# The small network and its border products in two batches, the first beside the last image's attention output; constant tables loaded as two parts by casting DMAs

## The chip, the cores and the metric

One core of a Trainium2 chip runs the whole program. The metric is the device time of one execution in microseconds, lower is better.

## The reference

Input x is [8, 128, 32, 32], f32. Two blocks follow each other (B = 8 images, C = 128 channels, N = 1024 positions):

```
# block 1, self-attention, per image
hn  = groupnorm(x, 16 groups) * norm_w + norm_b
q, k, v = conv1x1(hn; wq,bq), conv1x1(hn; wk,bk), conv1x1(hn; wv,bv)      # [128, 1024]
att = softmax(q^T k * C**-0.5)                                            # [1024, 1024]
x1  = x + conv1x1(v att^T; wp, bp)
# block 2, filter in the Fourier domain, on x1
xf   = fftshift(fft2(x1, ortho));  mag = mean over channels of |xf|
c    = mag[b, centre 7x7].reshape(8, 49)
par  = relu(c @ w1 + b1) @ w2 + b2                                        # the small network: 3 numbers an image
kern = an anisotropic Gaussian, 7x7, from par (an angle by arctan2, two widths by exp), over its sum + 1e-8
out  = real(ifft2(ifftshift(wr (kern * xf)))) + x1                        # zero-padded 7x7 convolution of xf
```

## The kernel before, in words

**Block 2 without a Fourier transform.** A circular convolution of the spectrum is a product in image space with a small function KHAT of the position; what zero padding changes is a correction of low rank. So for each image the kernel computes a feature row R = (projections of x1, 448 columns, and 50 columns with the real and imaginary parts of the central frequencies), then the 49 kernel values, KHAT as one product of the kernel with a cosine table, the correction through small matrices G and G3, Z = KHAT * X1 + correction, and the output as mix(Z) + X1.

**Precision.** Products are done in f32r on operands split into a high and a low part (QH and QL, ETH and ETL, SYH and SYL, ...): three passes, hi*hi, hi*lo, lo*hi. ACT rounds the high part off (a Copy into the f32r tile), and DVE or POOL subtracts it from the full value for the low part. This holds for the constant tables too: `ana` (features, tiles ANH and ANL), `syn` (SYH and SYL; its last 1024 columns are the cosine table), `gam` (border matrices GAMR and GAM3R, whose middle 32 rows are the low part). SP loads them in f32 and the engines split them.

**Engines and queues.** Every engine has its own program, in order; a wait on a semaphore holds all that is queued behind it. Names: `p_`, `a_`, `v_`, `g_` semaphores are raised by TensorE (PE), ACT, DVE, POOL, and `d_` by DMAs.

**Attention.** `attention(run, eng)` calls `image(b, cur, prev, nxt)` for b = 0, then in a loop for 1 to 6, then for 7, and a ninth time with cur = False for what is left of image 7. An image has eight tiles t of 128 queries: TensorE scores(t); DVE row maximum (L1080); ACT exponential (L814); DVE reciprocal of the row sum; POOL scale (L1446, 128x1024, in place in E); TensorE transposes (L450); ACT and DVE the high and low parts ETH (L823) and ETL (L1095); values(h, c) as products with V. Between the tiles stand the last steps of the image before: out_hi (L792) and out_lo (L1107), out_project, residual (DVE, T, L1116), x1_transposes (L495), XTH (L829) and XTL (L1100), keep_x1 (POOL, L1451), and at its end analysis(p) (`features` of 8 tiles, L504), whose result ACT copies to R (L921).

**The ninth call.** It has no scores. TensorE does values(7,0,2), transposes(7,7), values(7,0,3), values(7,1,0), out_project(7,0), values(7,1,1), x1_transposes(7,0), values(7,1,2), rt(0), values(7,1,3), out_project(7,1), four tiles of features, x1_transposes(7,1), the other four, and r3(0). ACT and DVE split the synthesis table in the meantime (L899, L900; L1226, L1230).

**The small network for all 8 images at once**, when R is complete: DVE squares and adds (L1246, L1248), ACT root, TensorE channel mean, DVE copy (C), TensorE hidden, DVE (HIDV), TensorE parameters, then `params` and `mlp_kernel` on DVE: some 33 operations on 49 x 8 to 49 x 32 elements of the tile ML (L1285 to L1346), each followed by a wait for its own result where the next one needs it, with a square root and an exponential on ACT in the middle. Then ACT the exponential of the kernel, TensorE its sum, DVE the quotient K (L1353), TensorE and both engines K3, the kernel in three parts. The borders are 14 products with 16 columns and 49 with 8:

```
for i in range(2 * NZ):
    ins = mm(bank(5)[0:CH, i * 2 * B:(i + 1) * 2 * B], GAMR[:, i * CH:(i + 1) * CH], K3[:], True, True)
ins.then_inc(s["p_g"], 1)
for i in range(NK):
    ins = mm(bank(4)[0:NK, i * B:(i + 1) * B], GAM3R[:, i * NK:(i + 1) * NK], K3[:, 0:B], True, True)
ins.then_inc(s["p_g"], 1)
```

DVE copies the first 14 (g_columns, L1361) and multiplies out G of image 0 (g_full, L1129) while the 49 run, then g3_columns (L1372).

**Synthesis.** `first()` and eight calls of `step(i, more)`, those for i = 1 to 4 in a loop. In a step TensorE does z(i,0), r3(i+1), z(i,1), v3(i+1), khat(i+1, 0 and 1), vt(i+1), mix(i,0), rt(i+2) (L526), mix(i,1). DVE does z_sum (L1161), g_lo, v3_lo, g_full, g3_copy (L1137), vt_lo, result(i,0) (L1170), rt_lo(i+2) (L1122), result(i,1), of which z_sum, v3_lo and vt_lo free TensorE. ACT does the high parts and the two copies of KHAT (L851), POOL KHAT * X1 (L1471), the low part of Z (L1477) and two copies for rt (L1461, L1463). TensorE's mix(i,1) goes to PSUM bank 7, and result(i,1) raises v_o to 2i + 2.

All matrix products have line L386, all plain low parts in the synthesis L1122, all plain ACT copies there L856.

## Time and profile before

| | |
|---|---|
| three runs | 463.03, 463.01, 457.34 us (median 463.01) |
| the profiled execution | 462.83 us |
| its span, first to last instruction | 461.0 us |
| busy in the span | PE 413.8, PEld 347.8, DVE 318.4, ACT 254.1, POOL 232.7 us |
| mean granted TensorE clock | 0.939 |

Rows and timeline entries give microseconds from the span's start; busy time of TensorE is at whatever clock was granted then, where 1.00 is 2.4 GHz and 0.50 is 1.2 GHz.

### The profile page before, as it was taken

Reading aid. Unit: us, or ns where it says so; the run is one execution under the profiler, and the core shown is the slowest. Engines: PE = TensorE matmul, PEld = TensorE weight load, DVE = VectorE, ACT = ScalarE, POOL = GpSimd, SP = SyncE. Lnnn points to the kernel's source line nnn. Section 1 sums busy time; section 2 is a strip of 40 time slices with the busy share of each in tenths; the row PEclk is TensorE's granted clock in tenths of the full one; section 3 lists DMA queues with packets and bytes.
Section 4 is the critical chain, followed back from the end, with each engine's and each line's share of the span. In section 5 each row is a group of like instructions: output and inputs, shape, how many; then the busy total and the mean of one; then the engine's idle time right before and its main releaser. Section 6 shows DMA issues by size and latency. Waiting matters only on the chain.

```text
span 461.0 us, 7023 instructions
## 1 busy us (share of the span) xinstructions
PE 413.8 (90%) x2263; PEld 347.8 (75%) x2263; DVE 318.4 (69%) x575; ACT 254.1 (55%) x450; POOL 232.7 (50%) x169
## 2 busy tenths in 40 slices
PE   2679899999999999999999999999965089999996
PEld 2458688888788888878888887888844088888884
DVE  3569689768849967894995889478353832577765
ACT  1557676656747665774665677467512312355551
POOL 0566457636816753781673477176013512467562
PEclk9989999999999999999999999999988555599999
DMA  6900100100000010010001001001150000111112
GB/s 173 376 30 2 46 1 0 47 0 0 11 35 0 0 45 0 0 45 0 0 0 45 0 0 46 1 1 43 71 132 0 0 1 1 45 46 45 67 71 91
DMA packets 6095, 17.54 MB, mean 38 GB/s; under 512 B 1633, under 2 KB 2273, under 8 KB 5857
## 3 DMA queue, kind: packets, MB, share of 16 engines
q1 hardware_dynamic: 4784, 16.70, 10.7%
q10 hardware_dynamic: 1296, 0.66, 0.5%
q8 instruction: 8, 0.13, 0.1%
q14 instruction: 7, 0.05, 0.0%
HBM read 13.16 MB, written 4.19 MB: 38 GB/s over the span
## 4 chain that ended last, share of the span: by engine, by line
PE 34%; issue 28%; POOL 25%; DVE 7%; ACT 3%; DMA 1%; POOLq 1%
PE PS L386 28%; POOL E L1446 17%; POOL VL L1436 4%; POOL HNL L1432 3%; PE PS L504 3%; PE PS L450 2%; POOL X L1451 1%; DMA X<-in_x 1%; DVE K L1353 1%; PE PS L526 1%; ACT E L814 1%; DVE NMX L1080 1%; DVE ETL L1095 1%; DVE ML L1285 1%; ACT ETH L823 0%
## 5 line engine op out<-in xcount | busy, mean ns | idle before, releaser
L1446 POOL TENSOR_TENSOR E<-E,RI 128x1024 f32<-128x1024 f32 x64 | 124.6, 1947 | 117.3 <-DVE RI L1085 117.3
L1080 DVE TENSOR_REDUCE NMX<-PS 128x1 f32<-128x1024 f32 x64 | 77.9, 1217 | 35.7 <-PE PS L386 35.2
L814 ACT ACTIVATE E<-PS,NMX 128x1024 f32<-128x1024 f32 x64 | 71.5, 1116 | 35.9 <-DVE NMX L1080 35.8
L823 ACT ACTIVATE ETH<-PS 128x512 fp32r<-128x512 f32 x128 | 69.5, 596 | 35.9 <-PE PS L450 35.5
L1095 DVE TENSOR_TENSOR ETL<-PS,ETH 128x512 fp32r<-128x512 f32 x128 | 82.1, 683 | 8.5 <-ACT ETH L823 7.7
L450 PE MATMUL PS<-MISC,E 128*128 128x128 f32 x512 | 67.6, 275 | 3.0 <-POOL E L1446 2.1
L450 PEld LDWEIGHTS PS<-MISC,E 128*128 128x128 f32 x512 | 59.4, 141 | 13.8 <-POOL E L1446 4.2
L386 PE MATMUL PS<-ETH,VH 128*128 128x512 f32 x128 | 55.2, 431 | 0.4 <-DVE ETL L1095 0.4
L386 PE MATMUL PS<-ETH,VL 128*128 128x512 f32 x128 | 50.6, 395 | 0.0
L386 PE MATMUL PS<-ETL,VH 128*128 128x512 f32 x128 | 50.4, 394 | 0.0
L386 PE MATMUL PS<-KH,QH 128*128 128x512 f32 x128 | 41.9, 409 | 2.1 <-ACT E L814 1.2
L386 PE MATMUL PS<-ETH 112*112 112x128 f32 (+5 forms) x128 | 41.8, 345 | 0.0
L386 PE MATMUL PS<-KL,QH 128*128 128x512 f32 x128 | 40.3, 396 | 0.0
L386 PE MATMUL PS<-KH,QL 128*128 128x512 f32 x128 | 40.1, 395 | 0.0
L386 PE MATMUL PS<-ETH,ETL 112*112 112x128 f32 (+3 forms) x112 | 36.3, 324 | 0.0
L1477 POOL TENSOR_TENSOR ETL<-E,ETH 128x512 fp32r<-128x512 f32 x14 | 18.6, 1325 | 24.8 <-ACT ETH L856 24.8
L386 PE MATMUL PS<-ETL,ETH 112*112 112x128 f32 (+3 forms) x96 | 30.7, 320 | 0.0
L386 PEld LDWEIGHTS PS<-ETH 112*128 112x128 f32 (+3 forms) x128 | 26.4, 211 | 4.0 <-DVE ETL L1122 0.5
L386 PE MATMUL PS<-HNH,WH 128*128 128x512 f32 x48 | 21.5, 447 | 8.4 <-DVE HNL L1066 3.7
L386 PEld LDWEIGHTS PS<-ETH,VL 128*128 128x128 f32 x128 | 24.3, 190 | 5.8
L386 PEld LDWEIGHTS PS<-KL,QH 128*128 128x128 f32 x128 | 24.1, 190 | 5.9 <-DVE KL L1074 0.6
L386 PEld LDWEIGHTS PS<-KH,QL 128*128 128x128 f32 x128 | 24.3, 190 | 5.4
(188 smaller groups left out, 791.5 us busy)
## 6 DMA issues: line engine op xcount, KB each, us to landing
XTF<-in_xt SPq DMA_DIRECT2D x8, 512.0 KB, 3.3
X<-in_x SPq DMA_DIRECT2D x7, 512.0 KB, 9.4
out<-X SPq DMA_DIRECT2D x7, 512.0 KB, 2.6
E<-in_gam SPq DMA_DIRECT2D x1, 1488.4 KB, 8.6
R<-in_ana SPq DMA_DIRECT2D x1, 1320.0 KB, 5.7
E<-in_syn SPq DMA_DIRECT2D x1, 752.0 KB, 4.3
X<-in_x ACTq DMA_DIRECT2D x1, 512.0 KB, 4.6
XTF<-in_syn SPq DMA_DIRECT2D x1, 512.0 KB, 5.3
```

The source lines that it names most:

```text
L386: return pe.matmul(o, a, b_, start=start, stop=stop)
L450: ins = pe.transpose(bank(ET_BANK + k)[:, j * P:(j + 1) * P], E[:, c0:c0 + P], eye)
L504: ins = pe.matmul(o[:, at:at + width], a, r, start=t == FIRST and n == 0, stop=t == LAST and n == 2, skip_group_check=True)
L526: ins = pe.transpose(bank(4)[0:CH, i * P:(i + 1) * P], RST[:, c * CH:(c + 1) * CH], eye)
L814: act.activation(E[:, (t % 4) * N:(t % 4 + 1) * N], s_bank(t), ACT.Exp, bias=NMX[:, t % 2:t % 2 + 1], accum_out=RS[:, t % 4:t % 4 + 1]).th ...
L823: act.activation(et[:, h, 4 * k:4 * k + 4, i * P:(i + 1) * P], bank(ET_BANK + k).rearrange("p (j n) -> p j n", j=4), ACT.Copy).then_inc(s[ ...
L1080: dve.tensor_reduce(NMX[:, t % 2:t % 2 + 1], s_bank(t), AX.X, ALU.max, negate=True)\
L1095: TT(etl[part], bank(ET_BANK + k).rearrange("p (j n) -> p j n", j=4), eth[part].bitcast(F32), ALU.subtract).then_inc(s["v_lo"], 1)
L1432: TT(HNL[:], XTF[:], HNH[:].bitcast(F32), ALU.subtract).then_inc(s["g_hl"], 1)
L1436: TT(VL[:, 4 * k:4 * k + 4, :], xt_half(k), VH[:, 4 * k:4 * k + 4, :].bitcast(F32), ALU.subtract).then_inc(s["g_vl"], 1)
L1446: TT(e, e, RI[:, t % 4:t % 4 + 1].broadcast_to([P, N]), ALU.mult)\
L1477: TT(ZL[:, d_], ZF[:, d_], ZH[:, d_].bitcast(F32), ALU.subtract)\
```

## The change

- The host computes the high and low parts of `ana` and `syn` and the three parts of `gam`. POOL loads each with a DMA from f32 to f32r: ANH and ANL after scale(0,2) of image 0; `gam` after image 7's last scale; SYH and SYL when values(7,0,3) are done. SP's loads of them and all splitting on ACT, DVE and POOL are gone. GAMR and GAM3R now lie over the Q and K tiles.
- The network, K3 and the borders are done for images 0 to 5 (batch 0) and for 6 and 7 (batch 1): `BATCHES = ((0, 6, 2, 3), (6, 2, 7, 7))`, where the last two numbers are the PSUM banks. Each batch has the full list of operations, with fewer columns.
- Batch 0: DVE's squares stand in image(7) at tile 6, after residual(6,1), ACT's root at that image's end, and the rest up to K3 in a new function `last()` of each engine, which takes the place of the ninth call. borders(0) open `first()`, with one semaphore at their end.
- Batch 1: squares end DVE's `last()`; centre stands in `first()`; hidden, parameters, norm and angle in step 0; sum and quotient in step 1; K3 in step 2; borders in step 3.
- The synthesis is written out without a loop.

The core of the diff. Batches:

```
+        BATCHES = ((0, 6, 2, 3), (6, 2, 7, 7))
```

TensorE, borders, `last()` and `step`:

```
+            def borders(k):
+                b0, n, _, at_ = BATCHES[k]
+                pe.wait_ge(s["v_k3"], k + 1)
+                pe.wait_ge(s["d_gam"], 16)
+                k3 = K3[:, 2 * b0:2 * (b0 + n)]
+                for i in range(2 * NZ):
+                    ins = mm(bank(at_)[0:CH, G_AT + i * 2 * n:G_AT + (i + 1) * 2 * n]
+                             if k else bank(at_)[0:CH, i * 2 * n:(i + 1) * 2 * n],
+                             GAMR[:, i * CH:(i + 1) * CH], k3, True, True)
+                for i in range(NK):
+                    ins = mm(bank(at_)[0:NK, G3_AT + i * n:G3_AT + (i + 1) * n],
+                             GAM3R[:, i * NK:(i + 1) * NK], k3[:, 0:n], True, True)
+                ins.then_inc(s["p_g"], 1)
+
+            def last():
+
+                p, pv, o = B - 1, LAST_PV_BANK, bank(LAST_U_BANK)
+                centre(0)
+                values(p, 0, 2)
+                hidden(0)
+                transposes(p, 7)
+                values(p, 0, 3)
+                parameters(0)
+                values(p, 1, 0, pv=pv)
+                out_project(p, 0, False)
+                values(p, 1, 1, pv=pv)
+                x1_transposes(p, 0)
+                values(p, 1, 2, pv=pv)
+                rt(0)
+                values(p, 1, 3, pv=pv)
+                pe.wait_ge(s["v_xl"], 2 * p + 1)
+                for t in TILE_ORDER[:TILES // 2]:
+                    features(t, o)
+                out_project(p, 1, False)
+                r3(0, after_mix=False)
+                x1_transposes(p, 1)
+                kernel_sum(0)
+                pe.wait_ge(s["v_xl"], 2 * p + 2)
+                for t in TILE_ORDER[TILES // 2:]:
+                    ins = features(t, o)
+                ins.then_inc(s["p_u"], 1)
+                kernel_thirds(0)
...
             def step(i, more):
+                if i == 0:
+                    hidden(1)
+                if i == 1:
+                    pe.wait_ge(s["v_o"], 2)
+                    kernel_sum(1)
                 z(i, 0)
                 if more:
                     r3(i + 1, after_mix=is_later(i))
+                if i == 0:
+                    parameters(1)
+                if i == 2:
+                    pe.wait_ge(s["v_o"], 4)
+                    kernel_thirds(1)
+                if i == 3:
+                    pe.wait_ge(s["v_o"], 6)
+                    borders(1)
                 z(i, 1)
...
+                if i == 0:
+                    pe.wait_ge(s["v_par"], 2)
+                if i == 1:
+                    pe.wait_ge(s["v_k"], 2)
+                if i == 2:
+                    pe.wait_ge(s["v_k3"], 2)
+                if i == 3:
+                    pe.wait_ge(s["v_g"], 6)
                 mix(i, 1, last=more == 0)
```

ACT, `last()` and the parts of `step`:

```
+            def last():
+                p = B - 1
+                et_hi(p, 7)
+                out_hi(p, 0)
+                misc_hi(XTH[:, 0:4, :], "p_xt", 2 * p + 1, "a_xh")
+                roots(0)
+                rt_hi(0)
+                out_hi(p, 1, LAST_PV_BANK)
+                act.wait_ge(s["g_vl"], 2 * B)
+                r3_copy(0)
+                misc_hi(XTH[:, 4:8, :], "p_xt", 2 * p + 2, "a_xh")
+                kernel_exp(0)
+                thirds_hi(0)
+                features_copy(p, LAST_U_BANK)
...
                     khat_copy(i + 1, 0)
                     khat_copy(i + 1, 1)
+                if i == 2:
+                    thirds_hi(1)
...
                     rt_hi(i + 2)
+                if i == 0:
+                    roots(1)
+                    kernel_exp(1)
```

DVE, image 7, `last()` and `step`:

```
+                    if not nxt and t == 6:
+                        squares(0)
...
+            def last():
+                p = B - 1
+                centre_copy(0)
+                hidden_copy(0)
+                et_lo(p, 7)
+                out_lo(p, 0)
+                params(0)
+                residual(p, 0)
+                mlp_norm(0)
+                misc_lo(XTL[:, 0:4, :], XTH[:, 0:4, :], "a_xh", 2 * p + 1, "v_xl")
+                rt_lo(0)
+                out_lo(p, 1, LAST_PV_BANK)
+                mlp_angle(0)
+                residual(p, 1)
+                misc_lo(XTL[:, 4:8, :], XTH[:, 4:8, :], "a_xh", 2 * p + 2, "v_xl")
+                kernel_of(0)
+                thirds_lo(0)
+                squares(1)
...
             def step(i, more):
+                if i == 0:
+                    hidden_copy(1)
+                if i == 1:
+                    kernel_of(1)
+                if i == 3:
+                    g_columns(1)
+                    g3_columns(1)
+                if i == 4:
+                    dve.wait_ge(s["v_g"], 6)
                 z_sum(i, 0)
                 if more:
                     g_lo(i + 1)
+                if i == 0:
+                    params(1)
                 z_sum(i, 1)
+                if i == 2:
+                    thirds_lo(1)
...
                 result(i, 0)
                 if more > 1:
                     rt_lo(i + 2)
+                if i == 0:
+                    mlp_norm(1)
+                    mlp_angle(1)
                 result(i, 1)
```

POOL, image 0, image 7's end and `last()`:

```
+                    if not prev and t == 2:
+                        pool.dma_start(ANH[:], anh).then_inc(s["d_ana"], 16)
+                        pool.dma_start(ANL[:], anl).then_inc(s["d_ana"], 16)
+                if not nxt:
+                    pool.wait_ge(s["p_s"], TILES * B)
+                    pool.dma_start(QK[0:K_ROWS, 0:GAM + NK * NK], gam).then_inc(s["d_gam"], 16)
+
+            def last():
+                p = B - 1
+                rst(0)
+                pool.wait_ge(s["p_pv"], 2 * p + 1)
+                pool.dma_start(SYH, syh).then_inc(s["d_syn"], 16)
+                pool.dma_start(SYL, syl).then_inc(s["d_syn"], 16)
+                pool.memset(G3S, 0.0).then_inc(s["g_g3z"], 1)
+                keep_x1(p, 0)
+                rst(1)
+                keep_x1(p, 1)
```

## Rows read from the trace of the kernel before

**Rows 1.** The page, busy tenths and granted TensorE clock in 40 slices of the span.
```profile
PE   2679899999999999999999999999965089999996
PEclk9989999999999999999999999999988555599999
```

**Rows 2.** Windows by stage: length, busy us of each engine, granted clock, DMA share, GB/s.
```profile
326.80:351.20 24.40, 18.29 (x91) 14.87 (x90) 9.31 (x11) 8.54 (x13) 2.11 (x5) 0.93 0.27 63
351.20:370.20 19.00, 3.21 (x36) 2.61 (x35) 13.37 (x43) 6.70 (x11) 9.39 (x4) 0.57 0.00 1
370.20:384.20 14.00, 13.39 (x87) 11.78 (x87) 4.57 (x10) 2.96 (x7) 1.26 (x1) 0.50 0.00 0
384.20:399.80 15.60, 15.60 (x55) 13.21 (x55) 6.49 (x10) 5.60 (x13) 7.83 (x9) 0.50 0.00 1
399.80:409.30 9.50, 9.50 (x55) 8.07 (x54) 6.20 (x10) 4.05 (x11) 4.71 (x4) 0.89 0.14 56
409.30:417.80 8.50, 8.50 (x55) 7.30 (x54) 6.55 (x11) 4.52 (x11) 5.71 (x7) 1.00 0.15 62
417.80:461.00 43.20, 38.64 (x237) 32.33 (x236) 29.43 (x46) 18.80 (x41) 22.83 (x23) 0.99 0.18 73
```

**Rows 3.** The chain of waits, rt(1) and rt(2): start us, length us, what.
```profile
383.52 0.85 PE PS L526 x4
...
397.90 0.85 PE PS L526 x4
```

**Rows 4.** Timeline of TensorE: start us, length us, operation, idle time before and its releaser.
```profile
337.49 1.11 PE L495 MATMUL PS<-MISC,T 128*128 128x128 f32 x4 [2.78 <-DVE T L1116]
...
370.19 2.78 PE L386 MATMUL PS<-K,ETL 96*112 96x16 f32 x14 [0.48 <-DVE K L1122]
372.82 4.22 PE L386 MATMUL PS<-K,ETH 96*49 96x8 f32 x49
```

**Rows 5.** Timeline of DVE: image 7, the network, and rt_lo(2) of step 0.
```profile
317.76 0.75 DVE L1116 SCALAR_TENSOR_TENSOR T<-PS,BV,X 128x512 f32<-128x512 f32 x1
319.03 1.23 DVE L1080 TENSOR_REDUCE NMX<-PS 128x1 f32<-128x1024 f32 x1 [0.52 <-PE PS L386]
...
355.84 2.32 DVE L1285 SCALAR_TENSOR_TENSOR ML<-ML 49x16 f32<-49x16 f32 x1
...
362.95 0.16 DVE L1346 TENSOR_TENSOR ML<-ML 49x8 f32<-49x8 f32 x1
...
399.42 0.69 DVE L1122 TENSOR_TENSOR ETL<-PS,ETH 112x512 fp32r<-112x512 f32 x1 [0.79 <-ACT ETH L856]
```

**Rows 6.** Timeline of POOL: a scale of image 7, and a split of the border table.
```profile
317.89 1.89 POOL L1446 TENSOR_TENSOR E<-E,RI 128x1024 f32<-128x1024 f32 x1 [0.77 <-DVE RI L1085]
...
354.65 3.48 POOL L1513 TENSOR_TENSOR ETL<-E,ETL 32x1568 fp32r<-32x1568 f32 x1 [6.83 <-ACT ETL L937]
```

**Rows 7.** Windows of a quarter microsecond in which the granted clock changes (columns as in Rows 2).
```profile
336.75:337.00 0.25, 0.00 (x0) 0.00 (x0) 0.25 (x1) 0.00 (x0) 0.00 (x0) 0.91 0.00 0
340.25:340.50 0.25, 0.25 (x3) 0.21 (x2) 0.00 (x0) 0.00 (x0) 0.00 (x0) 0.76 0.54 127
354.00:354.25 0.25, 0.21 (x2) 0.18 (x2) 0.00 (x0) 0.25 (x1) 0.00 (x0) 0.54 0.00 0
401.75:402.00 0.25, 0.25 (x3) 0.25 (x3) 0.00 (x0) 0.00 (x0) 0.00 (x0) 0.88 0.74 295
```

**Rows 8.** DMA issues with size and us to landing; SP's timeline of one issue.
```profile
E<-in_syn SPq DMA_DIRECT2D x1, 752.0 KB, 4.3
R<-in_ana SPq DMA_DIRECT2D x1, 1320.0 KB, 5.7
7.81 0.33 SPq L350 DMA_DIRECT2D R<-in_ana  x1
```

**Rows 9.** Timelines of DVE (v3_lo) and ACT (both copies of KHAT) in a step at full clock.
```profile
430.80 0.30 DVE L1122 TENSOR_TENSOR ETH<-PS,ETH 64x128 fp32r<-64x128 f32 x1
431.34 1.06 ACT L851 ACTIVATE E<-PS 128x512 f32<-128x512 f32 x2
```

429 lines of the change are left out of this document (199 added, 230 removed).

## The prediction

> **What bounds the kernel now.** I read the page's slices first, then windows by stage, then the chain of waits over the end. In the slices TensorE is full except at both ends and in one hole at four fifths of the span, and its granted clock is down in that hole and for four slices behind it [rows 1]. The windows cut the end at TensorE's own marks [rows 2]: 24.4 us of the last image's attention output (326.8 to 351.2), 19.0 us in which TensorE works 3.2 us while the small network runs, 14.0 us of border products and first preparations, then the eight synthesis steps: 15.6, 9.5 and 8.5 us for the first three and 43.2 us for the rest. A step of one shape costs 8.5 us at 2.4 GHz, and 14.4 us at 1.2 GHz (383.5 to 397.9) [rows 2, 3], with TensorE busy in all of it. So there are two prices: the network's hole, and the half clock behind it. In the attention loop (up to 326.8) TensorE is full, so nothing that is taken off ACT or POOL there is worth anything.
>
> When does the clock come back? It fell at 354.0, when TensorE had nearly stopped, and rose at 401.8 [rows 7], though TensorE was busy from 370 on [rows 2]. The borders' 63 narrow products didn't bring it back, nor did the first synthesis step; it rose only where both output mixes stood directly ahead of the next image's wide products. The earlier dip is other: it ended at 340.4, some 3 us after the wait of 2.78 us [rows 4, 7], with 128x512 products behind it.
>
> **The change, part by part** (times on the trace of before, then shifted).
>
> *The start.* The 1.32 MB load of the analysis table leaves SP's queue, and ACT's and POOL's splitting of it goes. Both copies lay beside projections and first scores; I count 0. POOL issues two loads of that size after scale(0,2) instead. No row shows a load issued by POOL; an issue on SP holds its queue for 0.33 us [rows 8], and the other end is 1.9 us each, as POOL's own large operation [rows 6]. The tables are wanted only one image later. I take 0.3 us, ends 0 and 2.
>
> *Squares of six images, inside image 7.* DVE does them right after residual(6,1), which ends at 318.5; the next row maximum started at 319.0 [rows 5]. Both inputs lie in SBUF, and POOL's scale holds from 317.9 to 319.8 [rows 6]. Such a pairing stands in the trace: the network's first DVE operation on SBUF, 49x16, took 2.32 us and ended when POOL's 3.48 us operation did [rows 5, 6]. So the squares wait to 319.8 and then take about 0.7 us; row maximum 7, the exponential, the ETL pieces and the last XTL piece shift by up to 1.9 us, and analysis(6) had followed XTL directly. Ends 0 and 1.9; I take 1.3.
> The Trainium skill, "SBUF — State Buffer", section "Who interferes with whom", says that a DVE instruction with two SBUF inputs contends with a GpSimd instruction that reads SBUF, and the one that comes second waits for all of it; by that rule the full 1.9 us would be paid, and the 2.32 us row agrees with it.
>
> *The last image's output with batch 0 in it.* Centre, hidden and parameter products add 0.9 us on TensorE before values(7,1,0). The 2.78 us wait for T [rows 4] goes, since DVE no longer splits the synthesis table. But residual(7,1) now stands behind mlp_angle(0) on DVE, and x1_transposes(1) waits for it. Counting down the queues: out_lo(7,1) ends at 340.25; the angle part is about two thirds of the 4.9 us that the network took from 358.2 to 363.1 without a neighbour [rows 5], 3.45 us; residual 0.75; so the transposes start at 344.5, where TensorE had come dry at 341.9. Another 1.2 us is lost until XTL. These two holes are like the one that dropped the clock at 337, so I take half clock from here: the last features 3.5 us instead of 1.9. kernel_sum and kernel_thirds hide or cost 0.8 us, K3's two copies 0.5 us. The borders begin at 351.3, against 370.2. The first two stretches, 43.4 us, become 24.5 (22.4 if the clock holds).
>
> *Borders(0) and preparations.* The same 63 products, with 12 and 6 columns instead of 16 and 8. They ran at 188 and 84 ns apiece at half clock (2.63 us for 14, 4.1 us for 49) [rows 4]; nearly all of that is not columns, so I keep 6.7 us, 3.4 to 3.7 at full clock. One semaphore stands at their end instead of two, so DVE's g_columns and g_full (1.2 us) no longer lie under the 49: v3 and vt come 1.0 us later. 14.0 becomes 15.0; I take 14.6 for a chance that the clock is up in a part of it.
>
> *Step 0.* Hidden and parameter products of batch 1 add 0.8 us. Then DVE's queue: rt_lo(2), mlp_norm(1), mlp_angle(1), result(0,1). TensorE waits for v_o = 2, that result, ahead of kernel_sum(1) and z(1,0); before, z(1,0) followed the mix at once. rt_lo ends at 400.1, 0.3 us behind the mix [rows 5]; the network needs 4.9 + 0.2 us again, result 0.7, kernel_sum 0.3: 6.6 us in which TensorE has nothing. Queued behind it are all products of step 1. 15.6 becomes 23.0.
>
> *Step 1.* A hole of 6 us starts it at half clock, and no pair of mixes with wide products behind comes before its end: 14.4 instead of 9.5.
>
> *Step 2.* thirds_lo(1) stands ahead of v3_lo(3) on DVE and waits for thirds_hi(1), which ACT does behind both K copies (to 432.4 in the like step; v3_lo was at 430.8) [rows 9]. vt's third group waits some 1.5 us. With 0.6 us for a clock that comes back only in z(2,0): 8.5 becomes 10.6.
>
> *Step 3.* borders(1), 63 products: 3.4 us at full clock, which is half of the 6.85 us from 370.19 to 377.04 [rows 4]. DVE's columns and z_sum hide behind z(3,1). They are as thin as those behind which the clock stayed down [rows 2]; if it falls here, the rest of the step pays 5 us more. Ends 0 and 5, I take 2.5. With the remaining steps 43.2 becomes 49.1.
>
> *Unrolling* removes loops in which the trace shows no gap on TensorE: 0.
>
> Sum of the changed stretches: 0.3 + 1.3 + 24.5 + 14.6 + 23.0 + 14.4 + 10.6 + 49.1 = 137.8 us, where before has 134.2. The profiled span was 461.0 and its time 462.8, so 1.8 lies outside: 461.0 + 3.6 + 1.8 = 466.4, say 466. The median shown is 463.0; the other run was 457.3, which fits a clock that comes back sooner in some executions. About 2% (9.3 us) is what a measurement here tells from no change.
>
> **Rivals.**
> (a) *The clock is up through borders(0) and step 0.* For: the dip at 337 lasted only 3.4 us. Against: the stretch of the network's thin products. Then 14.6 becomes 10.1, step 0 15.8 and the second borders cost 3.4 alone: 14.2 us less, 452. If besides step 1 stays up, 446.
> (b) *The hole in step 0 is filled or short*, for instance because the mixes bring the clock up ahead of it and it falls late; then step 1 costs 8.5 to 10: 460.
> (c) *Slower: late synthesis tables.* POOL may issue them only after p_pv = 15 (about 331), 1.3 and 0.8 MB; r3(0) waits for both and x1_transposes(1) is queued behind it. Loads of 1.32 and 0.75 MB took 5.7 and 4.3 us from SP [rows 8], so they land at about 342 with 1 us of issue, and 344.5 is the point from which it decides. If a casting load runs at half that rate they land at 352 to 353: 8 us more, 474.
> The Trainium skill, "DMA: Bandwidth & Descriptors", section "Anatomy of one DMA — SWDGE (gpsimd) path", gives 2.0 us plus bytes over 436 GB/s for such a load; by that estimate both have landed by 340 and (c) is nothing. No run here shows it yet.
> (d) *The change takes the hole out and nothing comes in its place* (step 0's wait is hidden by work I have put too early): 19 us off and, with the clock up, 435 to 445. Against it stands the queue order on DVE and the wait on v_o.
>
> **How the numbers follow.** Forecast 0.5; (a) 0.17; (b) 0.15; (c) 0.12; (d) 0.06. The forecast's own ends are 458 (features and second borders at full clock) and 471. Faster by over 2% is below 453.7: most of (a), and (d): 0.22. Slower by over 2% is above 472.3: (c) and the top of the forecast: 0.15. Range 452 to 473.
>
> **What the profile after would show.** TensorE's hole of 19 us gone, borders starting near 351 to 353; a wait of about 2.6 us for T ahead of the last x1 transposes; a wait of 6 us for the X result between steps 0 and 1; a clock at 0.5 from about 345 to beyond 400; DVE squares of 1 to 2 us beside POOL's scale; 63 narrow products inside step 3, and whether the clock falls behind them. It would be wrong above all if the clock rises before step 1, or if DVE gets through the second network before the mixes end.

## The result, and the profile after

The changed kernel takes 471.3 us (median of 4 runs, 470.2 to 472.2), the kernel before 462.4 beside it: ratio 1.028, 95% interval 1.021 to 1.035. It is slower: by 9 us between these medians, by some 13 by the ratio. Some executions of a kernel run at a lower granted clock and up to 3% longer than its others, and where that happened the medians below, like every ratio and interval, are of the others alone. The profiled execution took 470.16 us, with a span of 467.9.

The page, busy tenths and granted TensorE clock in 40 slices:

```profile
PE   2679999999999999999999999998977949899996
PEclk9989999999999999999999999999976775765999
```

Beside [rows 1] the network's deep hole is gone. The low clock isn't: before it was one block of six slices (0.8 twice, then 0.5 four times), now it is spread over eight of 0.5 to 0.7.

Windows by stage of the changed kernel (length, busy us of each engine with instructions, granted clock, DMA share, GB/s): last image, borders and preparations, step 0, step 1, step 2, step 3, step 4, the rest.

```profile
327.90:353.20 25.30, 21.48 (x119) 17.88 (x118) 12.10 (x50) 7.08 (x15) 3.89 (x9) 0.87 0.41 124
353.20:366.80 13.60, 11.62 (x93) 9.89 (x93) 5.37 (x14) 4.83 (x11) 1.50 (x2) 0.60 0.00 0
366.80:383.60 16.80, 10.61 (x62) 8.79 (x61) 11.99 (x47) 7.33 (x16) 7.43 (x9) 0.80 0.01 1
383.60:400.00 16.40, 16.36 (x58) 13.84 (x59) 6.76 (x13) 4.54 (x11) 5.94 (x6) 0.50 0.08 32
400.00:416.00 16.00, 14.75 (x79) 12.50 (x77) 8.24 (x12) 4.85 (x12) 6.06 (x6) 0.78 0.15 60
416.00:432.00 16.00, 16.00 (x99) 13.97 (x99) 5.90 (x12) 3.99 (x9) 5.93 (x6) 0.54 0.02 8
432.00:441.30 9.30, 9.30 (x54) 7.95 (x53) 5.90 (x10) 3.77 (x9) 4.17 (x4) 0.87 0.14 56
441.30:467.90 26.60, 22.02 (x132) 18.08 (x130) 16.68 (x27) 10.12 (x21) 11.80 (x11) 1.00 0.20 79
```

Against [rows 2]: the 43.4 us up to the borders have become 25.3. The window edges of the steps are rounded. From the first product of z(i,0) to that of z(i+1,0), steps 0 to 3 take 17.1, 15.6, 13.5 and 19.2 us, where before they took 15.6, 9.5, 8.5 and 8.6. They don't look alike: step 0 has 6 us in which TensorE is idle, step 1 is full at half clock, step 2 is at half clock in its second half, and step 3 is full, holds the second batch's 63 border products, and runs at half clock for most of its length.

TensorE's waits of the changed kernel (us in total, times, longest):

```profile
PE PS L393 <- DVE X L1234: 6.2, 1, 6.2
...
PE PS L501 <- DVE T L1180: 2.3, 1, 2.3
...
PE PS L393 <- DVE XTF L1201: 1.9, 1, 1.9
```

The 6.2 us are in step 0, ahead of the second batch's sum. Timeline of TensorE:

```profile
353.25 4.53 PE L393 MATMUL PS<-K,QK 96*112 96x12 f32 x63 [0.47 <-DVE K L1186]
...
383.64 0.33 PE L393 MATMUL PS<-ML,MISC 49*49 49x2 f32 x2 [6.23 <-DVE X L1234]
...
407.00 0.31 PE L393 MATMUL PS<-ETH 112*112 112x128 f32 x1 [1.25 <-DVE ETH L1186]
...
415.53 5.12 PE L393 MATMUL PS<-K,QK 96*112 96x4 f32 x63
```

and of VectorE in that hole, first and last of 32 rows of small instructions of the network, then result(0,1), for which TensorE waits:

```profile
378.00 0.26 DVE L1353 SCALAR_TENSOR_TENSOR ML<-ML 49x4 f32<-49x4 f32 x1
...
382.83 0.15 DVE L1417 TENSOR_TENSOR ML<-ML 49x2 f32<-49x2 f32 x1
382.91 0.68 DVE L1234 TENSOR_TENSOR X<-PS,X 128x512 f32<-128x512 f32 x1
```

Half-microsecond windows in which the granted clock changes from step 0 on (up, down, up, down, up, down, and the last one before it is up at 434.5):

```profile
369.50:370.00 0.50, 0.50 (x7) 0.50 (x5) 0.20 (x1) 0.00 (x0) 0.00 (x0) 0.86 0.00 0
379.50:380.00 0.50, 0.00 (x0) 0.00 (x0) 0.43 (x6) 0.26 (x2) 0.00 (x0) 0.88 0.00 0
400.00:400.50 0.50, 0.50 (x3) 0.40 (x2) 0.45 (x1) 0.00 (x0) 0.00 (x0) 0.64 0.00 0
407.00:407.50 0.50, 0.50 (x4) 0.50 (x4) 0.50 (x1) 0.00 (x0) 0.50 (x1) 0.69 0.00 0
414.00:414.50 0.50, 0.50 (x5) 0.46 (x4) 0.00 (x0) 0.00 (x0) 0.00 (x0) 0.98 0.00 0
417.00:417.50 0.50, 0.50 (x14) 0.50 (x13) 0.00 (x0) 0.00 (x0) 0.00 (x0) 0.93 0.00 0
434.00:434.50 0.50, 0.50 (x4) 0.50 (x4) 0.00 (x0) 0.00 (x0) 0.00 (x0) 0.50 0.59 238
```

Before these it fell at 345.7, in the wait for T, was up again from 352.5, and fell at 356.0, inside the first batch's 63 thin products. (A thin product is one with few columns, here 2 to 16.) Put beside the timelines, each fall has something in front of it: the hole (379.9), the wait of 1.25 us for the thirds (407.0), the second batch's thin border products (417.3). A fall doesn't need such a thing, though. In e1, the run below that has none of the three, the clock fell at 382.7, 393.0 and 420.3 for some 3 us each, with TensorE busy all the time:

```profile
379.00:382.00 3.00, 3.00 (x23) 2.50 (x22) 2.31 (x4) 1.93 (x5) 2.22 (x2) 1.00 0.25 98
382.00:385.00 3.00, 3.00 (x13) 2.45 (x13) 1.88 (x3) 0.74 (x3) 2.90 (x3) 0.62 0.00 0
```

So what stands in front of a fall is its cause only where a run without it keeps the clock up. The question for the experiments is which of them costs how much, and what the parts of the change are worth that aren't to be seen in this trace.

### The profile page after: what moved, and what is told of

Read it like the earlier page. It is cut to its first block, busy times and chain, and to the rows that moved or that the text cites. A ratio compares the mean times of both kernels' runs of the same rounds, so it can differ in the third digit from the quotient of the medians.

```text
span 467.9 us, 7056 instructions
## 1 busy us (share of the span) xinstructions
PE 428.6 (92%) x2340; PEld 360.1 (77%) x2340; DVE 317.5 (68%) x619; ACT 249.0 (53%) x450; POOL 221.8 (47%) x171
## 4 chain that ended last, share of the span: by engine, by line
PE 32%; issue 28%; POOL 25%; DVE 9%; ACT 4%; DMA 1%; POOLq 1%; DVEq 0%; ACTq 0%
PE PS L393 27%; POOL E L1560 16%; POOL VL L1553 4%; POOL HNL L1549 3%; PE PS L510 2%; DVE NMX L1144 2%; ACT E L866 1%; PE PS L457 1%; POOL X L1565 1%; PE PS L532 1%; DMA X<-in_x 1%; DVE ETL L1159 1%; ACT L976 1%; DVE STAT L1055 1%; DVE T L1180 0%
## 5 line engine op out<-in xcount | busy, mean ns | idle before, releaser
L393 PE MATMUL PS<-QK 128*128 128x512 f32 x384 | 100.2, 399 | 2.1 <-ACT E L866 1.2
L393 PEld LDWEIGHTS PS<-QK 128*128 128x128 f32 x384 | 71.3, 190 | 18.0 <-ACT E L866 1.6
L393 PE MATMUL PS<-ETH 112*112 112x128 f32 (+5 forms) x128 | 45.4, 374 | 1.2 <-DVE ETH L1186 1.2
L393 PE MATMUL PS<-ETH,ETL 112*112 112x128 f32 (+3 forms) x112 | 38.6, 345 | 0.0
L393 PEld LDWEIGHTS PS<-ETH 112*128 112x128 f32 (+3 forms) x128 | 29.0, 231 | 5.7 <-DVE ETH L1186 1.4
L393 PE MATMUL PS<-ETL,ETH 112*112 112x128 f32 (+3 forms) x96 | 32.9, 343 | 0.0
L909 ACT ACTIVATE ETH<-PS 112x512 fp32r<-112x512 f32 (+1 forms) x24 | 11.8, 490 | 34.1 <-PE PS L393 26.4
L1585 POOL TENSOR_TENSOR E<-E,X 128x512 f32<-128x512 f32 x16 | 20.5, 1299 | 18.9 <-ACT E L904 18.9
L1553 POOL TENSOR_TENSOR VL<-XTF,VH 128x512 fp32r<-128x512 f32 x16 | 20.6, 1290 | 14.7 <-ACT VH L844 14.7
L393 PEld LDWEIGHTS PS<-ETH,ETL 112*128 112x128 f32 (+1 forms) x112 | 25.6, 229 | 2.6
```

The source lines that it names most:

```text
L393: return pe.matmul(o, a, b_, start=start, stop=stop)
L909: act.activation(dst, src, ACT.Copy).then_inc(s[out_sem], 1)
L1553: TT(VL[:, 4 * k:4 * k + 4, :], xt_half(k), VH[:, 4 * k:4 * k + 4, :].bitcast(F32), ALU.subtract).then_inc(s["g_vl"], 1)
L1585: TT(KX[:, d_], KHAT[:, d_], X[:, bass.ds(n * N + h * HALF, HALF)], ALU.mult)\
```

## The experiments

The kernel before took 460.1 to 460.4 us beside the experiments. Where steps are given in microseconds, they are read from the profiled executions, from the first product of z(i,0) to that of z(i+1,0).

**e1, no second batch.** Everything that carries batch 1 is left out; images 6 and 7 take the border columns of images 0 and 1.

```diff
-                centre(1)
...
-                    kernel_thirds(1)
...
-                    borders(1)
...
-                col = n + BATCHES[k][0]
+                col = n % 6
```

> The changed kernel without anything of the second batch: no squares, centre, network, K3 or borders for images 6 and 7, which take the kernels of images 0 and 1 instead (so their output leaves out their own kernels). Theory T (the loss is the second batch: its hole in step 0, its thin products, and the half clock that they bring back): the steps run at 8.5 us once the clock is up, so the span falls from 468 to about 441, the first batch and the casting loads keeping their gain: time 440 to 446. Rival R (the loss lies in the casting loads, the written-out loop or the last image's rearranged queues): 460 or more. Rival W (only the waits and the added work count, not the clock): 6.2 + 1.3 + 5.0 + about 1 us less, 456 to 458.

Measured: 440.5 us, ratio 0.952 (0.950 to 0.955). By theory T. The first batch beside the attention, with the new loads, is a gain of some 20 us; the second batch takes 31 us and turns it into a loss.

**e4, the kernel before with its synthesis loop unrolled.**

```diff
-            step(0, 3)
-            with eng.Fori(1, B - 3) as i:
-                step(i, 3)
-            for i in range(B - 3, B):
+            for i in range(B):
                 step(i, B - 1 - i)
```

> The kernel before with the synthesis written out instead of a loop over steps 1 to 4. T: no change, 460 to 463. Rival R (instructions of written-out code come late): 2 us or more slower.

Measured: 460.0 us, ratio 0.998 (0.990 to 1.005). No effect of unrolling shows.

**e8, the kernel before with the casting loads alone.**

```diff
-            sp.dma_start(R[:, 0:UW], ana).then_inc(s["d_ana"], 16)
...
-            act.activation(ANH[:, 0:UA], R[:, 0:UA], ACT.Copy).then_inc(s["a_ur"], 1)
...
-            TT(ANL[:], R[:, 0:UW], ANH[:].bitcast(F32), ALU.subtract).then_inc(s["g_al"], 1)
...
+                        pool.dma_start(ANH[:], anh).then_inc(s["d_ana"], 16)
+                        pool.dma_start(ANL[:], anl).then_inc(s["d_ana"], 16)
```

and in the same way for syn and gam; gam lies in the Q and K buffers, as in the change.

> The kernel before with one part of the change: the constant tables arrive as two parts by GpSimd's casting transfers, so ScalarE's, VectorE's and GpSimd's splits of ana, syn and gam are gone; the network stays in one batch between attention and synthesis. Theory N (the loads are neither the loss nor a gain by themselves, since the splits lay beside other work save the gam part in front of the network): 460 to 463, ratio 0.995 to 1.000 beside 462.8. Rival G (the loads are a gain of their own that the second batch eats): the splits of SYN and GAM at the last image and in front of the borders go, 455 to 459. Rival R (the issues of 0.55 to 0.60 us on GpSimd and their packets hold image 0 and the last image up): 465 to 470.

Measured: 449.0 us, ratio 0.975 (0.967 to 0.983). More than any theory had. The waits of TensorE in e8:

```profile
PE PS L391 <- ACT ML L935: 6.0, 1, 6.0
...
PE PS L391 <- DVE K L1331: 0.7, 1, 0.7
```

In the kernel before they were 8.4 and 4.9 us, and the 2.78 us for T [rows 4] came ahead of them. The timelines say what went. First VectorE's quotient of the network in the kernel before, then, in the second fence, GpSimd's second split of the border table:

```profile
364.23 0.20 DVE L1351 RECIPROCAL ML<-ML 49x8 f32<-49x8 f32 x1
364.46 4.39 DVE L1353 TENSOR_TENSOR K<-ML 49x8 f32<-49x8 f32 x1
```

```profile
363.60 5.23 POOL L1513 TENSOR_TENSOR ETH<-E,ETH 32x2401 fp32r<-32x2401 f32 x1 [5.48 <-ACT ETH L944]
```

and the same quotient in e8, where GpSimd has nothing to split:

```profile
357.55 0.16 DVE L1331 TENSOR_TENSOR K<-ML 49x8 f32<-49x8 f32 x1
```

An instruction of 0.16 us took 4.39, and ended (368.85) when GpSimd's did (368.83). The network's other long one, 2.32 us beside GpSimd's 3.48 [rows 5, 6], takes 0.17 in e8. By the Trainium skill ("SBUF — State Buffer", "Who interferes with whom") VectorE's instruction with two SBUF inputs waits for all of a GpSimd instruction that reads SBUF and came first; both rows agree. So the splits weren't hidden: these two waited 6.4 us for GpSimd, T waited 2.8 us for VectorE's own split of the synthesis table, and with that wait the clock's dip at 337 [rows 7] went as well. Windows of e8: the last image from 327, the network, the borders, and what runs at half clock behind them:

```profile
327.00:347.00 20.00, 16.65 (x91) 13.52 (x89) 6.36 (x9) 6.15 (x11) 3.82 (x9) 1.00 0.47 145
347.00:359.00 12.00, 2.90 (x33) 2.29 (x32) 6.97 (x43) 2.99 (x8) 0.00 (x0) 0.59 0.01 1
359.00:367.00 8.00, 7.49 (x64) 6.99 (x64) 2.84 (x6) 1.32 (x3) 0.00 (x0) 0.50 0.00 0
367.00:390.00 23.00, 22.86 (x81) 19.06 (x82) 9.18 (x15) 7.34 (x17) 9.11 (x10) 0.50 0.00 1
```

So of e1's 20 us, 11.4 are the loads (460.4 to 449.0), and 8.6 more the first batch's place beside the attention (449.0 to 440.5, which also leaves out the network of two images).

**e2, the hole of step 0 filled** with 24 needless 128x128x512 products.

```diff
                 if i == 1:
+                    pe.wait_ge(s["v_z"], 2)
+                    for _ in range(24):
+                        mm(bank(0), WH[:, RI_, :], ZH[:, 0:HALF], True, True)
                     pe.wait_ge(s["v_o"], 2)
                     kernel_sum(1)
```

> The changed kernel with 24 needless 128x128x512 products on TensorE in its 6.2 us wait between steps 0 and 1, into a bank that the next z overwrites; nothing else. T: the clock stays at 2.4 GHz through the hole, step 1 takes 8.6 us instead of 15.6 and step 2 begins at full clock: 6 to 9 us faster than the changed kernel, 461 to 465. Rival W (work and waits alone): no gain, 470 to 472. Rival R: no gain either.

Measured: 467.5 us, ratio 1.014 (1.010 to 1.018), 3.7 us below the changed kernel and short of theory T. The executions scatter from 463.6 to 469.2. In the profiled one, the fastest, the clock rose at 371.7 and held through the hole, and step 1 took 8.6 us instead of 15.6. It fell at 402, behind the thirds' wait, and at 412.5, in the thin products, and steps 2 and 3 took 13.0 and 18.9 us, as without the fill (13.5 and 19.2). So the 7 us of step 1 were kept there. But 2.5 us had been lost ahead of step 0: the first batch's thin products took 6.87 us instead of 4.53, at half clock throughout. Why the other executions took longer is not shown.

**e3, the low parts of the second batch's thirds one place later on VectorE.**

```diff
-                if i == 2:
-                    thirds_lo(1)
...
                     g3_copy(i + 2)
+                if i == 2:
+                    thirds_lo(1)
```

> The changed kernel with thirds_lo(1) behind v3_lo(3), g_full and g3_copy in DVE's queue of step 2. T: the 1.25 us wait of TensorE in vt(3) goes; if that wait is also what dropped the clock at 407, step 2 falls from 13.5 to about 9.5 to 10: 468 to 470 with the wait alone, 465 to 467 with the clock. Rival R: no change, 471.

Measured: 467.9 us, ratio 1.015 (1.009 to 1.020), 3.3 below the changed kernel, with executions from 465.2 to 472.1. The wait of 1.25 us is gone, the clock stayed up from 399.4 to 413, and step 2 took 9.3 us instead of 13.5: the wait cost 4.3 us there, with the clock that fell behind it.

**e5, the second batch's network one step later**: norm behind result(0,1), angle behind result(1,1), sum, thirds and borders in steps 2, 3 and 4.

```diff
+                result(i, 1)
                 if i == 0:
                     mlp_norm(1)
+                if i == 1:
                     mlp_angle(1)
-                result(i, 1)
...
-                if i == 1:
-                    pe.wait_ge(s["v_o"], 2)
+                if i == 2:
+                    pe.wait_ge(s["v_o"], 4)
                     kernel_sum(1)
```

> The changed kernel with the second batch's network one synthesis step later: its norm goes behind image 0's product z*Re V (result(0,1)), its angle behind result(1,1), and the sum, the thirds and the borders to steps 2, 3 and 4. The 6.2 us in which TensorE waited for result(0,0) in step 0 lose their cause. Theory H (the hole is what costs, and it takes the clock with it: it fell at 379.9 inside the hole and stayed low through step 1): TensorE goes from z(0) into the mix at the clock that it had regained at 369.6, so 6 us go and step 1 takes some 9 to 10 us in place of 15.6; the waits for the thirds and the thin border products stay: 471.3 - 6 to 12 = 459 to 465. Rival V (the engine that is late there is VectorE, which has the same instructions to run): the hole comes back split over steps 1 and 2, and the time is within 2 us of 471. Rival C (TensorE's clock falls at the next bubble whichever it is): 6 us gained and no more, 465.

Measured: 471.8 us (two executions, 469.5 and 474.1), ratio 1.026 (1.015 to 1.037), the same as the changed kernel's. By rival V: in the profiled execution (480.2 us) the hole isn't in step 0 any more, but a wait of 4.8 us for ScalarE's exponential has come in front of the sum, now at the head of step 2, since the angle runs just ahead of it there too.

**e6, the second batch's 63 thin products in four parts** through step 3, the column copies behind V^T's.

```diff
-                    borders(1)
+                    borders_part(0)
                 z(i, 1)
+                if i == BAT:
+                    borders_part(1)
...
+                    if i == BAT:
+                        borders_part(2)
                     vt(i + 1)
+                if i == BAT:
+                    borders_part(3)
```

> The changed kernel with the second batch's 63 thin border products in four parts of 16 through step 3 (ahead of the two halves of z, behind the centre's share, behind V^T), and the copies of the columns behind V^T's. Theory T2 (63 thin products in one piece let the clock fall, which happened at 417.3 and lasted to 434.6, some 8 us of loss): between full-row products the clock stays up or comes back sooner, and the time is 463 to 467. Rival U (a thin product costs its own time wherever it stands, 63 in 5.0 us): 470 to 472, with the clock row the same. Rival L (the columns come late, and step 4's V^ waits for them): 472 to 476.

Measured: 464.8 us, ratio 1.013 (1.005 to 1.020), 6.5 below the changed kernel, by theory T2. The clock was low in step 3 from 423.7 to 427 only, instead of 417 to 434, and step 3 took 13.8 us instead of 19.2.

**e7, squares of the first batch out of image 7's scale**. TensorE's centre and hidden products and ScalarE's roots stand later too.

```diff
-                    if not nxt and t == 6:
-                        squares(0)
...
                     et_lo(b, 6)
+                if not nxt:
+                    squares(0)
```

> The changed kernel with the first batch's squares, magnitudes and centre ahead of the last image's stretch: VectorE squares behind the low part of image 7's second last weights, TensorE's centre product behind values(7,0,2). At the place of the change the square of 1.69 us and the sum of 0.60 us run beside the GpSimd scale (317.44 to 319.33). Theory S (VectorE is what image 7's end waits for there, 1.5 us by the comparison of the two traces): 469.5 to 470. Rival O (TensorE is behind anyhow at that place): 471, no difference that shows.

Measured: 468.3 us, ratio 1.017 (1.008 to 1.026): 3.0 us gained, 1.5 by the shift that the traces show. The rest is not placed and no larger than the scatter (464.8 to 470.5).

**e9, e8 with needless wide products in the network's holes:** 7 as shown, then 24, 3 and 2 ahead of the later waits, and one behind every seventh thin product.

```diff
+            for _ in range(7):
+                mm(bank(0), WH[:, RI_, :], HNH[:, 0:HALF], True, True)
             pe.wait_ge(s["a_mag"], 1)
```

> e8 (the kernel before with casting loads alone) plus needless full-row 128x128x512 products where TensorE waits in the network: 7 ahead of the centre, 24 ahead of the sum, 3 and 2 ahead of the thirds and the borders, one behind every seventh thin border product. In e8 TensorE waits 6.0 us for ScalarE's exponential there and its clock reads 0.50 from 349 to 390.5, through the borders and step 0. Theory C (what keeps the clock down is that TensorE lacks wide products for this stretch): the clock stays at full through preparations and step 0, which at half clock take some 20 us of products, so 7 to 10 us less, minus some 2 us of needless work on the path: 441 to 444 us. Rival D (the clock falls in the border products or behind any of the waits all the same): 449 to 452.

Measured: 447.3 us, ratio 0.969 (0.965 to 0.974). Filled holes hold the clock (1.00 up to 357), but it fell in the thin border products, at 363, though a wide product stood behind every seventh. It came back at 376.7 instead of 390. By the profiled executions (445.6 against 451.5) that is 6 us, by the medians 1.8: between the theories.

**e10, e3 + e6 + e7 on the changed kernel, and e11, e10 with e2's fill.**

> The changed kernel with e3, e6 and e7 together: the low parts of the second batch's thirds behind g3_copy, its border products in four parts through step 3, the squares of the first batch at image 7's end. Theory A (each takes away a cost of its own: 3 us of squares and order, 1.2 us of wait with the clock fall of step 2, the low clock of step 3): 457 to 460, what is left over e1 being the hole of 6.2 us with step 1 at half clock, and the work itself. Rival B (the clock pays one low stretch whichever bubble is left): 463 to 465.

> e10 with e2's 24 needless full-row products in the hole of step 0. Theory A: the hole's 6.2 us stay as time, but step 1 runs at full clock as in e2 and no later wait makes it fall, so 7 us less than e10: 450 to 453. Rival B (as in e2, where the clock rose early and fell again in step 2 behind the wait of 1.2 us, and only 3 us were left): within 3 us of e10.

Measured: e10 462.1 us, ratio 1.006 (0.999 to 1.012), which is 9.2 off the changed kernel where the three alone add up to 12.8: in e10 the clock is low from 378.7 to 399.2, as without them, and again from 416.2 to 423.2, and step 3 takes 15.1 us against 13.8 in e6. It lies between theories A and B. e11 455.0 us, ratio 0.986 (0.982 to 0.990): 7.1 below e10, nearer to theory A. In its trace step 1 takes 8.6 us instead of 15.6, the same 7 us that the fill gave in e2's.

**e12, no border products in the second batch.** Images 6 and 7 take other images' columns, all else stays.

```diff
-                if i == 3:
-                    pe.wait_ge(s["v_o"], 6)
-                    borders(1)
```

> The changed kernel without the second batch's border products and the copies of their columns; images 6 and 7 take the border columns of images 0 and 1, while the rest of the second batch's network stays. It sizes the borders alone. Theory T2: 63 thin products of 5.0 us, and the low clock from 417.3 to 434.4 behind them (some 8 us), so 458 to 460 beside 471.3. Rival U (the products' time only): 466. What e12 leaves above e1's 440.5 is then the hole, the wait of the thirds and their falls of the clock: 18 to 20 us by T2, 26 by U.

Measured: 460.6 us, ratio 1.003 (0.997 to 1.009). Step 3 takes 8.8 us instead of 19.2, with the clock up in it:

```profile
417.00:417.50 0.50, 0.50 (x7) 0.50 (x6) 0.24 (x1) 0.00 (x0) 0.00 (x0) 1.00 0.33 131
```

So the 63 thin products of 5.1 us cost 10.4, nearest to theory T2. 20 us are left over e1.

**e13 and e14, without the chain of small instructions.**

```diff
+                if k == 1:
+                    TT(m(ML_N2), m(ML_P), m(ML_P), ALU.mult).then_inc(s["v_n2"], 1)
+                    return
...
+                    TT(m(ML_E), m(ML_NR), m(ML_LAM), ALU.add).then_inc(s["v_ex"], 1)
```

> The changed kernel without the second batch's chain of small VectorE instructions for norm and angle (36 of them from 378.0 to 382.9 us, ahead of the second half of result 0); two multiplications take their place, so the kernels of images 6 and 7 are not the reference's. All other instructions of the second batch stay. Theory H (the hole of 6.2 us in step 0 and the fall of the clock in it): the hole shrinks to 1 or 2 us, the clock stays up through step 1 (7.85 us in e2 where it did, 15.6 where not), and the wait for the thirds or the thin products let it fall later: 471.3 - 5 - 3 to 8 = 458 to 463. Rival P (the clock falls at the same place for want of wide products, as in e5): 5 us only, 466.

> e13 together with the three mends of e10 (463.1). By theory H nothing of the second batch is left that stops TensorE longer than 1 or 2 us: 63 thin products of 5 us at half clock, 16 other small products, and the copies: 448 to 452, e1's 440.5 plus that work and one low stretch. By rival P: 458.

Measured: e13 465.9 us, ratio 1.009 (1.003 to 1.014); e14 457.9 us, 0.997 (0.991 to 1.002). Both as by rival P, but it isn't shown by them: the hole shrank to 3.5 us only. (The chain left out is the 32 rows of the trace above, not 36.) Windows of e13, the hole and step 1:

```profile
376.50:380.50 4.00, 0.48 (x4) 0.23 (x2) 1.82 (x5) 2.56 (x6) 1.32 (x3) 0.85 0.00 0
380.50:396.00 15.50, 15.50 (x56) 13.18 (x56) 6.13 (x12) 4.27 (x10) 5.94 (x6) 0.50 0.09 34
```

The clock fell again in 3.5 us of idle time, and step 1 cost 15.6 us again. What makes these 3.5 us is the order on TensorE: the sum stands ahead of z(1,0) and waits for result(0,1), chain or no chain.

**e15 to e18, the sum later in step 1.** e15 moves it behind V^T, ahead of mix(1,0), and its quotient on VectorE to ahead of result(1,0); e16 is that without the chain; e17 and e18 are both with the three mends.

```diff
-                if i == 1:
-                    pe.wait_ge(s["v_o"], 2)
-                    kernel_sum(1)
                 z(i, 0)
...
                     vt(i + 1)
+                if i == 1:
+                    pe.wait_ge(s["v_o"], 2)
+                    kernel_sum(1)
                 mix(i, 0, last=more == 0)
```

> The changed kernel with the second batch's sum moved within step 1, from ahead of z(1,0) to ahead of mix(1,0), and its quotient on VectorE from the step's start to ahead of result(1,0). TensorE no longer stops for result(0,1) at the step's start: it goes on with z(1,0), r3, z(1,1) while VectorE runs its chain of small instructions. Theory W (the place of the wait makes the hole): most of 6.2 us goes, some of it comes back where VectorE, 5 us behind, is late for V^T or the sums of z; with the clock up through step 1: 459 to 463. Rival Q (VectorE's chain makes it: the wait only moves): 468 to 471.

> e15 and e13 together: the sum late and the chain of 36 small instructions left out, two multiplications in its place (the kernels of images 6 and 7 are not the reference's). Now neither cause of a hole is there. Theory W and Q alike: no wait over 1 us in steps 0 and 1, full clock from 369 to the thirds' wait of step 2: 456 to 459. If the clock falls in step 1 all the same (rival P, want of wide full-row products), 463 to 466.

> e15 with the three mends of e10 (463.1 with them alone). Computes the reference. Theory W: 451 to 455, under the kernel before (461), though not under e8 (449). Rival Q: 460 to 463.

> e16 with the three mends. Of the second batch only its products (63 thin ones and 19 small ones), its copies and ScalarE's roots are left, nothing waits: e1's 440.5 plus 5 to 8 us: 446 to 449. If a low stretch through step 1 or 3 stays: 452 to 456.

Measured: e15 462.3 us, ratio 1.007 (1.001 to 1.014); e16 459.6, 1.000 (0.992 to 1.008); e17 453.6, 0.989 (0.980 to 0.997), from two executions only, while its other two took 463.3 and 464.5; e18 447.0, 0.975 (0.968 to 0.982). Windows of e18, which has neither cause of a hole: step 0, step 1, and what follows:

```profile
368.50:382.00 13.50, 13.10 (x89) 11.05 (x87) 9.43 (x20) 7.76 (x18) 6.59 (x7) 1.00 0.09 35
382.00:396.00 14.00, 13.67 (x83) 11.38 (x84) 10.99 (x19) 7.67 (x18) 10.56 (x11) 1.00 0.11 44
396.00:405.50 9.50, 9.50 (x103) 8.74 (x101) 4.85 (x8) 3.18 (x8) 4.72 (x6) 1.00 0.14 55
405.50:412.00 6.50, 6.50 (x36) 5.53 (x35) 4.37 (x9) 1.85 (x5) 1.72 (x3) 0.74 0.17 66
```

The clock rises at 368.2, and now stays up to 405.6, after the spread borders. Theory W holds, with e15, e17 and e18 in its ranges and e16 0.6 us above: where the wait stands makes most of the hole. Step 0 takes 10.0 us in e15 instead of 17.1. In e15 VectorE's chain still shows, as a wait of 3.0 us for ScalarE's high part in step 1, with the clock low from 384.7 to 394.7. In e16 that wait is gone, and step 1 takes 10.0 us instead of 15.8. The chain is the smaller share: of the 12 us between the changed kernel and e16, moving the sum alone gives 9 (e15), leaving out the chain alone 5 (e13).

The steps of synthesis in the profiled executions, us:

| run | step 0 | step 1 | step 2 | step 3 |
|---|---|---|---|---|
| before | 15.6 | 9.5 | 8.5 | 8.6 |
| changed | 17.1 | 15.6 | 13.5 | 19.2 |
| e2, hole filled | 16.7 | 8.6 | 13.0 | 18.9 |
| e3, thirds late | 16.7 | 15.6 | 9.3 | 18.2 |
| e6, thin products spread | 16.9 | 15.6 | 13.5 | 13.8 |
| e12, no second borders | 16.8 | 15.6 | 13.5 | 8.8 |
| e16, sum late, no chain | 10.1 | 10.0 | 11.8 | 19.2 |
| e18, e16 with the three mends | 10.2 | 10.0 | 9.1 | 13.7 |
| e1, no second batch | 10.1 | 10.1 | 10.0 | 8.7 |

Each edit moves the step that it is aimed at and leaves the others nearly as they were. Three steps of e1 are above 8.5 us because the clock comes up only inside the first, and falls for some 3 us in the next two.

The account of the second batch, in medians:

| from | to | us | what |
|---|---|---|---|
| changed kernel 471.3 | e16 459.6 | 11.7 | hole in step 0 and step 1 at half clock |
| e16 | e18 447.0 | 12.5 | the three mends: thirds' wait, thin products in one piece, squares |
| e18 | e1 440.5 | 6.6 | the second batch's own work: 63 thin products (4.1 us in four parts), 18 small ones, copies |

Of the versions that leave nothing out, e8 is the fastest without needless work (449.0 us): the change's loads with the old, single batch. It beats the kernel before by 2.5% and the changed kernel by about 5%. e9 with its needless products is at 447.3; their intervals overlap. A batch of six images beside the attention is worth 8.6 us more (e1), but I found no place for the other two that costs less than that: the best is e17, 13.1 us above e1.

## Why the prediction was right or wrong

The time of 471.3 us lies in the range, but the forecast of 466 with "no change" as likeliest is wrong: the kernel is slower by 2.8%. That the number is only 5 us off is luck: step 0 came out 6 us too dear and the steps behind it 10 us too cheap. The trace of before, to which the sum was added, is of an execution of 462.8 us, 2.5 above what that kernel took beside the experiments. Measured between the same marks, in the profiled execution:

| term | predicted | measured |
|---|---|---|
| start, squares | 0.3 + 1.3 | -0.45 + 1.5 |
| last image's stretch | 24.5 | 25.35 |
| borders(0) and preparations | 14.6 | 13.45 |
| step 0 | 23.0 | 17.0 |
| step 1 | 14.4 | 15.8 |
| step 2 | 10.6 | 13.55 |
| step 3 and the rest | 49.1 | 54.8 |
| sum | 137.8 | 141.0 |

*Start and squares.* Right. The stretch up to image 7 was 0.45 us shorter. POOL's issues took 0.54 to 0.74 us each, within the bounds, and hid. The square beside POOL's scale took 1.69 us and ended 0.3 us behind it; the same operation on 400 columns took 0.57 us in e8 with POOL idle. The Trainium skill's rule ("SBUF — State Buffer", "Who interferes with whom"), that the later one waits for all of the other, agrees with it. Moving the squares away (e7) shortened the traced execution by 1.5 us, so the term was on the path.

*The last image.* Right: the wait for T was 2.3 us against 2.6, behind mlp_angle(0) as said, and the clock fell at 345.7. Rival (c), late synthesis tables, did not happen: both were issued at 332.9 and 333.4 and landed 5.7 and 7.0 us later, ahead of r3(0), which began at 342.7 without a wait. The Trainium skill's price for a casting load ("DMA: Bandwidth & Descriptors", "Anatomy of one DMA — SWDGE (gpsimd) path") gives an estimate of 5.0 and 3.8 us for these two; the trace agrees within 1 us for the first, but not for the second, which took 7.0 right behind it and landed at 340.4.

*Step 0.* The hole was right in place, cause and length: 6.23 us for X against 6.6. Its price was wrong. I took the clock to be down from 345 to beyond 400, because in the kernel before it "rose only where both output mixes stood directly ahead of the next image's wide products". It was up from 352.5 to 356.0, and rose again at 369.6, in z(0), as at 368 to 372 in every other run with the changed kernel's queues but e5 (387.3). So step 0 was 6 us cheaper. My rule came from one rise in one trace. Rival (a), with the clock up through borders(0) and step 0, came true in part; its 452 did not, since the clock fell again in the hole.

*Steps 1 to 3: the step that failed.* The miss that made the kernel slower is here, in "if it falls here, the rest of the step pays 5 us more. Ends 0 and 5, I take 2.5". The same picture of a single long stretch at half clock made the later steps too cheap. From the hole on the clock fell three times and came back three times. I had allowed step 2 its wait (1.5 us, measured 1.25) and 0.6 us of clock; e3 shows that the wait brings the clock down: without it step 2 takes 9.3 us instead of 13.5. For the second borders I took those 2.5 on top of 3.4; they cost 10.4 by e12, more than the upper end of 8.4, with the clock low for 17 us up to step 4. Step 2 and step 3 with the rest are 8.65 us above the forecast, which is more than the whole error. Step 1 was undersized by an error of counting: 14.4 us is the distance of rt(1) to rt(2), and that of a whole step at half clock is 15.6.

*What was not asked.* The prediction summed stretches and never priced the loads apart from the network. The rows were at hand: I took the 2.32 us row for the squares' price and left its neighbour of 4.39 us unread, on the quotient that the hole ended with. The loads are worth 11.4 us (e8), the first batch's place some 9, and the second batch loses 31. With these three numbers in hand the change would have been seen as two gains and a loss larger than both, and the doubt would have gone to the loss. Rival (d)'s point, that nothing comes in place of the hole, is e1 without the second batch: 440.5, in its range of 435 to 445. But over half of that gain is the loads, which (d) doesn't name, so the number is partly luck.

## What to carry to other kernels

Splitting a serial piece of work into batches to hide the first adds the waits and the small work of the second: price that as if it were the only change (here 6.6 us of work alone, 31 with its waits and the clock). Here waits of 1.25 and 6.2 us on TensorE cost 4 and 13 us, since the clock fell behind them, so look where in TensorE's own order the waiting instruction stands before shortening the work that it waits for (e15 against e13). Measure the parts of a change by themselves: here the plain part, tables that arrive already split, was all of the gain that the fastest version without needless work kept.

## What the runs showed of the hardware

- Gains that come from the clock need not add up. e3, e6 and e7 give 12.8 us alone and 9.2 together, with a scatter of 3 to 7 us within each run: in e10 the clock was low for 7 us in step 3, in e6 for 3.5.
- 63 thin products in one piece (96x49 and 96x112 against 2 to 16 columns) took the clock down while TensorE was busy without a gap. It fell inside them or within 1.5 us in the changed kernel (417.3), e2, e3, e7, e13, e15 and e16, and stayed up there in e12, which leaves them out. In e9 it fell at 363, with a 512-column product behind every seventh. In four parts among wide products the low stretch was 3.5 us in e6, 7 in e10 and e17.
- The clock also fell for some 3 us with TensorE full, no wait and no thin product near: at 382.7, 393.0 and 420.3 in e1, 400.0 in e11, 433.4 in e3, each time at the first output mix, behind the 128-column products of V^T. So e6's and e18's low stretches of 3 us at the same place in the step (423.7 and 405.6) may be no matter of the thin products. Why it falls there is open.
- A thin product's time hardly depends on its columns: 63 with 16 and 8 columns took 6.85 us at half clock [rows 4], 63 with 12 and 6 took 6.87 us in e2. In the changed kernel those with 12 and 6 took 4.5 us since the clock was up for the first 2.8 us of them.
- VectorE's 49x8 operation in SBUF took 4.39 us beside a GpSimd operation of 5.23 us, and 0.16 us without it. It began 0.86 us after GpSimd's and ended with it, as the one of 2.32 us did: the price is what is left of GpSimd's operation, whatever VectorE's own work.
- Idle stretches of 1.25 us (step 2 of the changed kernel) and 3.5 us (step 0 of e13) were each followed or met by a fall of the clock that lasted 7 us or more: 407.3 to 414, and 379.3 to 396. Their length alone doesn't decide: in e8 TensorE waited 1.56, 1.41 and 1.47 us between 338 and 349 (the second of them below), and the clock stayed up until 349.3.

```profile
343.50:344.00 0.50, 0.00 (x0) 0.00 (x0) 0.28 (x1) 0.19 (x1) 0.44 (x2) 1.00 0.00 0
```
